# Spare identity products among TensorE's steps in the first iteration of a Mamba-2 and feed-forward kernel, and a new hand-written order of that iteration on four engines

## What is computed

```
x = x + layernorm(mamba2(layernorm(x)))
x = x + layernorm(ffn(layernorm(x)))
mamba2(u): z, xBC, dt = split(u @ in_proj)          # 256 -> 1288
           x, B, C = silu(causal_conv(xBC, 4 taps))
           dt = softplus(dt + dt_bias)
           Y = scan over the sequence with decay exp(dt*A), state 8 x 64 x 128
           y = rmsnorm((Y + D*x) * silu(z)) * norm_weight
           return y @ out_proj                       # 512 -> 256
ffn(x):    Wg, Wu, Wd = 4-bit codes from a table, times a scale for each block of 32
           return (gelu(x @ Wg.T) * (x @ Wu.T)) @ Wd.T   # 256 -> 2048 -> 256
```

## Time and profile before

| | |
|---|---|
| time, median of 3 runs | 967.86 us (967.83 to 968.83) |
| the profiled execution's own time | 965.19 us |
| its span, first to last instruction | 963.1 us |
| PE busy | 880.5 us (91%) |
| DVE busy | 751.7 us (78%) |
| ACT busy | 614.1 us (64%) |
| POOL busy | 355.0 us (37%) |
| mean granted TensorE clock | 0.972 of full |

### The profile page before, as it was taken

How to read it: one execution, slowest core, us unless ns; L and a number is a source line. 1 busy time by engine, 2 the same in 40 slices (tenths; PEclk the granted TensorE clock), 3 DMA queues, 4 the chain that set the end, 5 groups by cost and what they waited for, 6 DMA issues and landing times.

```text
span 963.1 us, 17495 instructions
## 1 busy us (share of the span) xinstructions
PE 880.5 (91%) x6304; PEld 767.2 (80%) x6304; DVE 751.7 (78%) x2031; ACT 614.1 (64%) x1031; POOL 355.0 (37%) x342
## 2 busy tenths in 40 slices
PE   3256979999999999999999999999999999999987
PEld 3136878978897887988898897888888898888886
DVE  5989889877888697887978788787978878786232
ACT  5767777866749394765858385774858485673222
POOL 2030515253342516243442515243442525344323
PEclk9579999999999999999999999999999999999999
DMA  7502010200101010100102010110102010010000
GB/s 228 178 1 56 1 56 2 67 1 21 37 13 66 1 56 2 57 21 13 45 12 67 1 56 1 36 43 13 45 13 67 1 56 1 23 45 1 1 23 11
DMA packets 19205, 34.57 MB, mean 36 GB/s; under 512 B 2480, under 2 KB 11440, under 8 KB 19120
## 3 DMA queue, kind: packets, MB, share of 16 engines
q1 hardware_dynamic: 18256, 33.44, 10.8%
q10 hardware_dynamic: 864, 0.03, 0.1%
HBM read 29.14 MB, written 4.33 MB: 35 GB/s over the span
## 4 chain that ended last, share of the span: by engine, by line
PE 63%; DVE 15%; ACT 13%; issue 5%; POOL 3%; DMA 1%; SPq 0%; POOLq 0%; ACTq 0%; DVEq 0%
PE fb L1082 28%; PE db L1082 14%; PE mb L1082 10%; DVE xc L890 3%; PE mb L1191 3%; ACT L710 3%; PE mb L1182 2%; POOL hl L588 2%; ACT hid L710 2%; PE mb L1172 2%; ACT xc L670 2%; PE mb L1197 1%; ACT xc L663 1%; DVE st L1007 1%; ACT lmat L652 1%
## 5 line engine op out<-in xcount | busy, mean ns | idle before, releaser
L588 POOL TENSOR_TENSOR hl<-hid,hl 128x512 fp32r<-128x512 f32 (+1 forms) x144 | 182.7, 1273 | 336.1 <-ACT hl L717 336.1
L1082 PE MATMUL fb<-x1t,wg 128*128 128x512 f32 (+1 forms) x864 | 215.9, 386 | 3.2 <-DVE x1t L993 2.7
L1082 PE MATMUL fb<-x1t,wu 128*128 128x512 f32 (+1 forms) x864 | 203.2, 371 | 16.3 <-ACT hid L710 16.3
L1082 PE MATMUL db<-wd,hl 128*128 128x256 f32 x1536 | 217.5, 291 | 0.7 <-POOL hl L588 0.7
L1082 PEld LDWEIGHTS db<-wd,hl 128*128 128x128 f32 x1536 | 196.2, 191 | 14.7 <-issue 9.8
L1082 PEld LDWEIGHTS fb<-x1t,wu 128*128 128x128 f32 x864 | 150.6, 190 | 51.5 <-ACT hid L710 25.4
L1082 PEld LDWEIGHTS fb<-x1t,wg 128*128 128x128 f32 x864 | 147.6, 191 | 36.4 <-issue 11.6
L710 ACT ACTIVATE hid<-fb 128x512 f32<-128x512 f32 (+1 forms) x144 | 78.5, 550 | 135.1 <-PE fb L1082 119.5
L890 DVE SCALAR_TENSOR_TENSOR xc<-raw,cw,xc 128x256 f32<-128x256 f32 x288 | 135.7, 539 | 6.8 <-ACT xc L663 4.8
L999 DVE TENSOR_TENSOR hid<-fb,hid 128x512 f32<-128x512 f32 (+1 forms) x144 | 90.1, 626 | 60.7 <-PE fb L1082 34.4
L558 POOL TENSOR_TENSOR rs<-ve,neg_half 128x1 f32<-128x1 f32 (+2 forms) x89 | 61.9, 696 | 175.6 <-DVE ve L792 68.5
(11 more groups left out here) (141 smaller groups left out, 1294.1 us busy)
## 6 DMA issues: line engine op xcount, KB each, us to landing
lmat<-rows SPq DMA_DIRECT2D x32, 512.0 KB, 4.5
xin<-in_u SPq DMA_DIRECT2D x16, 256.0 KB, 2.7
out<-xb SPq DMA_DIRECT2D x16, 256.0 KB, 2.3
wg_raw<-in_packed SPq DMA_DIRECT2D x4, 256.0 KB, 12.4
wg_raw<-in_scales SPq DMA_DIRECT2D x4, 256.0 KB
wu_raw<-in_packed SPq DMA_DIRECT2D x4, 256.0 KB, 12.1
wu_raw<-in_scales SPq DMA_DIRECT2D x4, 256.0 KB
wd_raw<-in_packed SPq DMA_DIRECT2D x4, 256.0 KB, 11.9
```

What stands on the lines that cost most here:

```text
L588: pool.tensor_tensor(hl[:, hs, n % 2, 1, :], hid[:, hs, n % 2, :], hl[:, hs, n % 2, 0, :].bitcast(F32), ALU.subtract).then_inc(s["lo"], 1)
L1082: last = pe.matmul(ps, lhs(a, k), rhs(b, k), start=start and n == 0, stop=stop and n == len(todo) - 1, skip_group_check=check)
```

## The change

A new PE step `warm` multiplies the identity by the constant triangle `upto` twice, into `db[0]`, which nothing reads in that iteration. It waits for nothing but, the first time, the constants. There are 24 of them in PE's list of the first iteration. The four lists of that iteration are new: each has the same steps as before (108 on PE beside the new ones, 145 on ACT, 154 on DVE, 46 on POOL) in another order. `ORDER` and `LAST` are as they were.

```diff
 FIRST = {
     "pe": """
-        xt:1 ip:3 ip:4 z:3 z:4 z:5 ip:5 cs:1 xtr:2 ct:1 gb:1 yo:2 st:2 xt:0> yd:2 xtr:3 yt:2 yo:3 yd:3 out:2
-        yt:3 st:3 out:3 z:0> z:1> ip:0> ip:1> x1t:1 cs:0> ip:2> z:2> gu:0 gu:1 ct:0> gb:0> xtr:0> yo:0> gu:2
-        dn:0 st:0> yd:0> gu:3 dn:1 xtr:1> yt:0> gu:4 gu:5 dn:2 yo:1> out:0> yd:1> gu:6 xt:1> yt:1> dn:3 dn:4
-        st:1> gu:7 out:1> gu:8 ip:3> ip:4> z:3> z:4> dn:5 dn:6 gu:9 cs:1> z:5> ct:1> ip:5> xtr:2> dn:7 gb:1>
-        yo:2> dn:8 gu:10 st:2> xt:0>> yd:2> gu:11 xtr:3> yt:2> dn:9 gu:12 out:2> yo:3> gu:13 dn:10 yd:3> gu:14
-        st:3> dn:11 yt:3> gu:15 out:3> z:0>> z:1>> dn:12 x1t:0> dn:13 ip:0>> ip:1>> x1t:1> z:2>> ip:2>> dn:14
-        dn:15""",
+        warm:0 xt:1 ip:3 warm:1 z:3 z:4 warm:2 ip:4 ip:5 cs:1 ct:1 z:5 warm:3 xtr:2 gb:1 warm:4 yo:2 warm:5
+        xt:0> st:2 warm:6 yd:2 warm:7 xtr:3 yt:2 warm:8 yo:3 out:2 yd:3 warm:9 yt:3 warm:10 st:3 out:3 z:0>
+        warm:11 z:1> warm:12 warm:13 ip:0> ip:1> warm:14 warm:15 cs:0> x1t:1 warm:16 ip:2> warm:17 z:2> warm:18
+        ct:0> warm:19 gu:0 gu:1 warm:20 xtr:0> gb:0> gu:2 yo:0> warm:21 warm:22 gu:3 warm:23 dn:0 st:0> yd:0>
+        gu:4 dn:1 yt:0> xtr:1> dn:2 gu:5 out:0> yo:1> gu:6 yd:1> dn:3 xt:1> st:1> dn:4 yt:1> dn:5 ip:3> out:1>
+        gu:7 gu:8 z:3> z:4> ip:4> gu:9 dn:6 dn:7 cs:1> ip:5> z:5> gu:10 dn:8 gu:11 dn:9 xtr:2> ct:1> yo:2> gb:1>
+        gu:12 xt:0>> dn:10 st:2> yd:2> gu:13 xtr:3> yt:2> dn:11 gu:14 yo:3> dn:12 out:2> yd:3> gu:15 x1t:0>
+        yt:3> st:3> dn:13 out:3> z:0>> z:1>> dn:14 dn:15 ip:0>> ip:1>> x1t:1> ip:2>> z:2>>""",
     "act": """
-        wi_split:0 wi_z:0 xn_split:1 rates:0 taps:3 taps:4 dq:0 dq:1 dl:0 dq:2 dt_bias:1 gate:3 gate:4 dq:3 dq:4
-        taps:5 dq:5 silu:3 dl:1 dl:2 silu:4 dq:6 gate:5 dq:7 dq:8 silu:5 wo_split:0 dl:3 dl:4 exps:1
...
+        wi_split:0 wi_z:0 xn_split:1 rates:0 dq:0 taps:3 dq:1 silu:3 dl:0 dq:2 taps:4 dq:3 dq:4 dt_bias:1 gate:3
+        dl:1 gate:4 dl:2 dq:5 taps:5 dq:6 dq:7 dl:3 gate:5 silu:4 dq:8 silu:5 wo_split:0 dq:9 exps:1
...
     "dve": """
-        stats1:1 xn:1 wi_split:0 xn_split:1 rates:0 conv:3 wo_split:0 dt_bias:1 dq:0 scale:0 dq:1 scale:1 dq:2
-        scale:2 dl:0 stats1:0> dq:3 scale:3 conv:4 dq:4 dq:5 softplus:1 xn:0> dq:6 dq:7 scale:4 decays:1 conv:5
-        dq:8 scale:5 dl:2 wo_lo:0 dl:3 xdt:2 sums:1 dl:1 gb_copy:1 yoff:2 decayed_products:2 scale:6 state:2
...
+        stats1:1 xn:1 xn_split:1 wi_split:0 dq:0 rates:0 scale:0 conv:3 dt_bias:1 dq:1 stats1:0> dq:2 conv:4
+        wo_split:0 dl:0 scale:1 scale:2 dq:3 dq:4 softplus:1 dq:5 decays:1 scale:3 dq:6 scale:4 conv:5 scale:5
+        xn:0> dl:1 scale:6 dq:7 sums:1 wo_lo:0 dl:2 gb_copy:1 xdt:2 decayed_products:2 yoff:2 xn_split:0>
...
+        yt_split:1> dl:6 inter:6 dq:11 stats2:1> scale:11 inter:7 ln2:1> dt_bias:1> conv:3> softplus:1> dl:8
+        conv:4> decays:1> inter:8 inter:9 stats1:0>> conv:5> dl:10 inter:10 sums:1> dl:9 xdt:2> gb_copy:1>
...
+        state:3> inter:15 x1_split:0> x1n:2> stats2:3> dt_bias:0>> ln2:3> fin:0 x1n:3> conv:0>> x1_split:1>
+        softplus:0>> ln4:0""",
...
+            def warm(i, par, k):
+
+                if k == 0:
+                    pe.wait_ge(consts_ready, 1)
+                for n in range(2):
+                    pe.matmul(db[0][:, CH * n:CH * n + CH], ident[:], upto[:], start=True, stop=True)
```

More of the change, by code:

```diff
@@ L109 @@
-        st:3> dn:11 yt:3> gu:15 out:3> z:0>> z:1>> dn:12 x1t:0> dn:13 ip:0>> ip:1>> x1t:1> z:2>> ip:2>> dn:14
-        dn:15""",
-    "act": """
-        wi_split:0 wi_z:0 xn_split:1 rates:0 taps:3 taps:4 dq:0 dq:1 dl:0 dq:2 dt_bias:1 gate:3 gate:4 dq:3 dq:4
-        taps:5 dq:5 silu:3 dl:1 dl:2 silu:4 dq:6 gate:5 dq:7 dq:8 silu:5 wo_split:0 dl:3 dl:4 exps:1
[L114 to L125, removed]
@@ L126 @@
-    "dve": """
-        stats1:1 xn:1 wi_split:0 xn_split:1 rates:0 conv:3 wo_split:0 dt_bias:1 dq:0 scale:0 dq:1 scale:1 dq:2
-        scale:2 dl:0 stats1:0> dq:3 scale:3 conv:4 dq:4 dq:5 softplus:1 xn:0> dq:6 dq:7 scale:4 decays:1 conv:5
-        dq:8 scale:5 dl:2 wo_lo:0 dl:3 xdt:2 sums:1 dl:1 gb_copy:1 yoff:2 decayed_products:2 scale:6 state:2
[L130 to L140, removed]
@@ new lines @@
+        gu:7 gu:8 z:3> z:4> ip:4> gu:9 dn:6 dn:7 cs:1> ip:5> z:5> gu:10 dn:8 gu:11 dn:9 xtr:2> ct:1> yo:2> gb:1>
+        gu:12 xt:0>> dn:10 st:2> yd:2> gu:13 xtr:3> yt:2> dn:11 gu:14 yo:3> dn:12 out:2> yd:3> gu:15 x1t:0>
+        yt:3> st:3> dn:13 out:3> z:0>> z:1>> dn:14 dn:15 ip:0>> ip:1>> x1t:1> ip:2>> z:2>>""",
+    "act": """
+        wi_split:0 wi_z:0 xn_split:1 rates:0 dq:0 taps:3 dq:1 silu:3 dl:0 dq:2 taps:4 dq:3 dq:4 dt_bias:1 gate:3
+        dl:1 gate:4 dl:2 dq:5 taps:5 dq:6 dq:7 dl:3 gate:5 silu:4 dq:8 silu:5 wo_split:0 dq:9 exps:1
+        decay_sums:4 decay_sums:5 decay_matrix:4 gb_copy:1 decay_matrix:5 decay_sums:6 decay_matrix:6
+        xn_split:0> decay_sums:7 decay_matrix:7 square:2 yt_split:2 dl:4 yt_split:3 dl:5 square:3 dt_bias:0>
+        gate:0> taps:0> taps:1> gate:1> dq:10 x1_split:1 silu:0> taps:2> dl:6 dl:7 silu:1> gelu:0 gelu:1 gate:2>
+        split:0 silu:2> split:1 decay_sums:0> gelu:2 decay_sums:1> exps:0> decay_matrix:0> gb_copy:0>
+        decay_matrix:1> gelu:3 decay_sums:2> split:2 decay_sums:3> square:0> gelu:4 split:3 yt_split:0>
+        decay_matrix:2> split:4 decay_matrix:3> gelu:5 dq:11 dl:8 dl:9 split:5 gelu:6 xn_split:1> yt_split:1>
+        split:6 square:1> taps:3> gelu:7 dl:10 dl:11 gelu:8 split:7 dt_bias:1> gelu:9 gate:3> gate:4> taps:4>
+        taps:5> silu:3> split:8 silu:4> split:9 gate:5> gelu:10 gelu:11 silu:5> exps:1> split:10 decay_sums:4>
+        decay_sums:5> gb_copy:1> decay_matrix:4> decay_matrix:5> split:11 decay_sums:6> xn_split:0>> gelu:12
+        decay_sums:7> gelu:13 square:2> split:12 yt_split:2> decay_matrix:6> decay_matrix:7> gelu:14 split:13
+        yt_split:3> square:3> x1_split:0> gelu:15 split:14 split:15 gate:0>> taps:0>> gate:1>> taps:1>>
+        x1_split:1> dt_bias:0>> taps:2>>""",
@@ new lines @@
+    "dve": """
+        stats1:1 xn:1 xn_split:1 wi_split:0 dq:0 rates:0 scale:0 conv:3 dt_bias:1 dq:1 stats1:0> dq:2 conv:4
+        wo_split:0 dl:0 scale:1 scale:2 dq:3 dq:4 softplus:1 dq:5 decays:1 scale:3 dq:6 scale:4 conv:5 scale:5
+        xn:0> dl:1 scale:6 dq:7 sums:1 wo_lo:0 dl:2 gb_copy:1 xdt:2 decayed_products:2 yoff:2 xn_split:0>
+        state:2 ydiag:2 decayed_products:3 dl:3 yt_split:2 xdt:3 yoff:3 stats2:2 ydiag:3 ln2:2 yt_split:3
+        state:3 dq:8 scale:7 stats2:3 dt_bias:0> x1n:2 ln2:3 softplus:0> x1n:3 conv:0> dl:4 decays:0> x1_split:1
+        conv:1> conv:2> inter:0 sums:0> scale:8 inter:1 xdt:0> dq:9 dl:5 gb_copy:0> scale:9 inter:2 dq:10
+        stats1:1> decayed_products:0> yoff:0> state:0> inter:3 ydiag:0> xn:1> scale:10 inter:4 yt_split:0> dl:7
+        xdt:1> stats2:0> decayed_products:1> inter:5 yoff:1> ln2:0> ydiag:1> x1n:0> xn_split:1> state:1>
+        yt_split:1> dl:6 inter:6 dq:11 stats2:1> scale:11 inter:7 ln2:1> dt_bias:1> conv:3> softplus:1> dl:8
+        conv:4> decays:1> inter:8 inter:9 stats1:0>> conv:5> dl:10 inter:10 sums:1> dl:9 xdt:2> gb_copy:1>
+        xn:0>> inter:11 yoff:2> decayed_products:2> state:2> xn_split:0>> x1n:1> ydiag:2> inter:12 dl:11
+        inter:13 yt_split:2> xdt:3> decayed_products:3> yoff:3> inter:14 stats2:2> ydiag:3> ln2:2> yt_split:3>
+        state:3> inter:15 x1_split:0> x1n:2> stats2:3> dt_bias:0>> ln2:3> fin:0 x1n:3> conv:0>> x1_split:1>
+        softplus:0>> ln4:0""",
@@ L141 @@
     "pool": """
[L142 to L145, removed]
+        stats1:1 wi_split:0 stats1:0> xdt:2 yoff:2 xdt:3 yoff:3 stats2:2 ln2:2 stats2:3 ln2:3 split:0 split:1
@@ L146 @@
+        xdt:0> stats1:1> yoff:0> split:2 split:3 split:4 xdt:1> stats2:0> yoff:1> split:5 ln2:0> split:6
+        stats2:1> split:7 split:8 split:9 stats1:0>> split:10 xdt:2> ln2:1> yoff:2> split:11 split:12 xdt:3>
+        yoff:3> split:13 stats2:2> ln2:2> split:14 split:15 stats2:3> ln2:3> fin:0""",
 }
@@ L1240, in _ @@
             drive(pe, "pe", dict(xt=xt, ip=ip, cs=cs, ct=ct, z=z, gb=gb_, xtr=xtr, yo=yo, yd=yd, st=st, yt=yt_, out=out_,
-                           x1t=x1t_, gu=gu, dn=dn), identity)
+                           x1t=x1t_, gu=gu, dn=dn, warm=warm), identity)
 def kernel(**inputs):
```

## The result

The changed kernel takes 960.33 us, median of 4 runs (960.11 to 961.48), against 967.85 (966.44 to 968.83) for the kernel before: -7.5 us, ratio 0.9932 with a 95% interval of 0.9917 to 0.9947. I had forecast 961.5 with a range of 956.5 to 969.0.

A forecast was written before the change was run, and what follows sets the result against it. TensorE paces the loop, DVE has least slack before it. Terms sum to -5.1 us; leaned two to one against a walk's -8.9 this gives -6.4, so 961.5 us from the 967.86 median, range 956.5 to 969.

The forecast's parts named there:

- The bound: TensorE paces the loop, so its first product `gu:0` moves the end; before it DVE has least slack, 26.6 us.
- My sum: First iteration, all terms added: -3.9 - 1.7 - 1.7 - 0.9 + 1.8 + 1.3 = -5.1 us.
- a walk that ended at -8.9: New lists followed step by step to the loop's `gu:0`: 170.3 instead of 179.23 us, leaving out small gaps and collisions.
- Head, term -3.9: Start to `conv:0>`: less DVE work before `sums:1`, so `conv:0>` comes at 78.5 against 82.36 us.
- The cause that I gave for the start: On DVE `xn_split:1` ahead of `wi_split` delays `ip:3` to 12.8 and `conv:3` to 17.3 us.
- Tail, terms -1.7 and -1.7: From 82 to 141 us: removed waits less new ones, -1.7 us; clock no longer falling from 140 to 150, -1.7.
- the +1.3 us for ACT's tables: Three more ACT table loads; half of the two where ACT is dense charged, +1.3 us.
- Pairs, +1.8 and -0.9: `warm:21` to `warm:23` before ready work cost +1.8 us; higher clock between 50 and 80 us gains 0.9.
- The one around 95 us I leave: Clock drop around 95 us expected to remain, since the wait for the first `gelu` stays; no gain counted.
- the first rival: Step-by-step estimate holds in full, or pairs raise the clock from 50 us and around 95: about 958.5 us, chance 0.25.
- The rival on the other side: `warm:11` to `warm:23` run before ready TensorE work and are paid: +4 us, near 972, chance 0.15.
- my sign of a wrong end: Entry into the loop: TensorE waiting before `gu:0` for `x1_split:1>` would show the end was predicted wrongly; no size given.

The follow-up runs named there:

- the set with POOL's wait: Kernels whose POOL `wi_split` also waits for DVE's two `wi_split` instructions: old lists 965.63 us, new lists without pairs 962.25, new lists with pairs 960.31.
- the new head followed by the old tail: New lists up to about 75 us, remaining steps in old order, no pairs, added wait in POOL's `wi_split`, against the kernel before: 962.14 us, ratio 0.9948.
- the new tail: Old lists up to about 75 us, remaining steps in new order, no pairs, added wait in POOL's `wi_split`, against the kernel before: 964.11 us, ratio 0.9965.
- the transposes: Changed kernel with each product of a pair made a transpose of `upto` through the identity: 959.55 us, ratio 0.9919 to the kernel before.
- `wi_split` first: Changed kernel with `wi_split` back ahead of `xn_split` on DVE and POOL's `wi_split` waiting for DVE's: 959.69 us, ratio 0.9919 to the kernel before.

## Why the prediction was right, point by point

**The bound** was read rightly. The loop's product `gu:0` carries most of the difference of the two traces, 2.7 of 3.3 us, and behind it every trace takes the same time within 0.8 us. Within the first iteration DVE's idle time is what fell, from 26.6 to 23.6 us.

**The time came out near, the sum less so.** In the set with POOL's wait the -7.05 us between the kernel before and the new lists with pairs split into -1.7 (the collision), -3.4 (the order) and -1.9 (the pairs). My sum had no collision, -6.0 for the order and +0.9 for the pairs; the forecast then leaned to a walk that ended at -8.9. The errors are of both signs and partly cancel. That the median came within 1.2 us of the forecast is in part luck: in the two traces `gu:0` moved by 2.7 us and not by the 6.4 of the forecast, and the rest of the 7.5 us is in the difference between the profiled executions and their medians.

**Head, term -3.9:** measured -3.5 (-3.3 by the ratios), and its marks hold: `sums:1` predicted at 48.3, found at 48.55; `decayed_products:2` 52.3 and 52.68; `conv:0>` 78.5 and 78.94. The mechanism is the one I gave: weight work put off from before `sums:1` falls in DVE's later waits. The cause that I gave for the start was only half right. `ip:3` was later than I said, by the collision (13.66, not 12.8). `conv:3` (17.3 predicted, 18.23 found) owes about 1 us to that and hangs for the rest on the landing of the first codes, through ACT's list: with `ip:3` at 10.19 it is still at 17.70.

**Tail, terms -1.7 and -1.7:** these failed. The wait before `xtr:2>` went and the clock stays up behind it, as I said, but the new head followed by the old tail takes the same time as both new, within what can be told. I counted the removed wait as a gain of its own. DVE is busy 9.69 of 10 us behind it, which suggests that its list needs the time anyway; no run shows this by itself. Nor does one test the +1.3 us for ACT's tables alone: the new tail, with two of the three loads more, is neither faster nor slower. `cs:1>` came at 132.64, where it had been before (132.80), though the head was over 3 us ahead. Two waits that the walk lacked are in the trace on the way: `sums:0>` behind the rows that come back from memory (1.74) and `st:0>` behind POOL (1.78).

**Pairs, +1.8 and -0.9:** the sum has the wrong sign, since they give 1 to 2 us with the new order. `warm:21` to `warm:23` do stand before ready work. What I had wrong is "The one around 95 us I leave": the pairs of products keep the clock at 1.00 there. That is a part of the first rival, which I gave 0.25. How much of the gain comes from it is not shown. The old lists with pairs have a higher clock there too and gain nothing, and the transposes gain as much at 0.85. The rival on the other side, pairs paid before ready work, did not come: with them the wait before `gu:1`'s second half is 0.60 us and not 2.93 (2.42 in the new order without pairs), so much of the cover was indeed used up, but at full clock.

**The other signs.** `gb:0>` is 3.2 us ahead and not 4, the wait before `xtr:2>` is gone, the clock is 1.00 from 140 to 150 us, and DVE is idle 23.6 us. TensorE does wait before the loop's `gu:0` for `x1_split:1>`, my sign of a wrong end, but only 0.22 us. The first rival's "about 958.5" doesn't follow from its own terms: -8.5 and -8.9 on 967.86 give 959.4 and 959.0.

The Trainium skill (TensorE: Matmul & The Clock Gate, Part 4) says that work in transpose mode doesn't count as busy in the same way as products. The run with transposes neither bears this out nor excludes it: its clock near 95 us is 0.85, where products gave 1.00, but a pair of transposes is also shorter, 0.38 us against 0.60.

**Offset to the median.** I set the forecast 2.67 us above the profiled execution, as if this were a constant. It belongs to the old order: the changed kernel's profiled execution was above its median. The likely cause is the collision, absent from the profiled execution, since with POOL's wait the old lists' median is 965.63, near the 965.19 of that execution. That the collision happens in the runs that have no trace is inferred from this gain and from the one trace with the old lists in which it is seen.

**What stays open.** Which instructions lose the time in the longer runs of the old order beyond the collision, and where on the way to the loop the pairs give their 1 to 2 us. The two fastest variants, with `wi_split` first (959.69) and with transposes (959.55), have intervals that overlap that of the changed kernel, so no version here is shown to beat it.

## What to carry to other kernels

Where one engine's list sets the time, putting its uncritical work off pays when that work lands in waits that the engine has later. Moving a step forward only to do the same work behind it pays nothing: `conv:3` 2.9 us earlier left the time as it was. A wait removed on another engine further on brought nothing that could be told here either. Spare products gained 1 to 2 us in one order and nothing in another; test them together with the order they are meant for, and don't take a higher clock for a shorter time. Before a profiled execution is used as the baseline, compare it with the median: a difference of 2.7 us was as large as a third of the effect here. One pair of traces is not enough to show where a gain of 1 or 2 us comes from, when two executions differ by as much.

## What the runs showed of the hardware that was not expected

A DVE subtraction of 16 columns took 2.31 us when it began 0.29 us behind a POOL subtraction on the same weights, and 0.17 us otherwise; a wide one took 2.96 instead of 1.76. Both end about as if they had waited for POOL's instruction to finish. For the small one, 9.00 + 2.57 and 9.29 + 2.31 are both 11.6. For the wide one, POOL is done at 9.51 + 2.40 = 11.91, 1.76 more is 13.67, and it ended at 13.51. `xn_split`, one of whose inputs lies in PSUM, ran inside the same POOL instruction at 9.95 and took its usual 0.69. The Trainium skill (SBUF — State Buffer, "Who interferes with whom") says that a DVE instruction with two inputs in SBUF contends with a GpSimd one that reads SBUF, that the port pair they share is locked exclusively, and that the order of issue decides who blocks. The traces agree.

The granted clock reads 1.00 over the first 20 us of the changed kernel. Yet its first pair takes 1.20 us, at 2.88 us, as at half clock, and its first twelve products of 256 columns take 2.93. Twelve such products at a clock of 0.50 take 2.90 (28.09 us in the trace of before), and 1.43 at 1.00. For the first products of a kernel the durations are to be read and not the clock.
